# Graph network on one core: GpSimd's gathers wait for VectorE's additions and are spaced by progress

## What is computed

```python
q = (h @ Wq.T + bq)[dst]; k = (h @ Wk.T + bk)[src]; v = (h @ Wv.T + bv)[src]      # by head
alpha = jnp.sum(q * k, axis=-1) / sqrt(D_HEAD)
ex = jnp.exp(alpha - segment_max(alpha, dst)[dst])
a = ex / (segment_sum(ex, dst)[dst] + 1e-16)
out = segment_sum((a[:, :, None] * v).reshape(-1, f), dst)
# then a gate with x_r = h @ Ws.T + bs, a layer norm, and a feed-forward of 512 with gelu
...
msg = silu(concat([x[src], x[dst], rbf]) @ mw1 + mb1) @ mw2 + mb2                  # last pass
agg = segment_sum(msg, dst) / max(cnt, 1)
out = silu(concat([x, agg]) @ uw1 + ub1) @ uw2 + ub2                              # and layer norms
```

## Time and profile before

| | |
|---|---|
| median of 3 runs | 5662.24 us (5661.85 to 5665.38) |
| profiled execution: its span | 7864.5 us |
| its time beside the span | not shown; the page gives the span alone |
| busy share of the span | PE 58%, VectorE 52%, GpSimd 49%, ScalarE 35% |
| DMA | 536.12 MB, of it 490.24 MB by GpSimd's queue |
| chain that ended last | PE 27%, unknown 25%, issue 20%, VectorE 17% |

### The profile page before, as it was taken

One profiled execution on the slowest core, in us unless ns is written; L12 is line 12 of the kernel. 1 busy time (PEld: TensorE's weight loads), 2 busy tenths in 40 slices (PEclk: granted clock), 3 DMA queues, 4 the chain that ended last, 5 costly groups with the idle time before them and its releaser, 6 DMA issues.

```text
span 7864.5 us, 105863 instructions
## 1 busy us (share of the span) xinstructions
PE 4591.8 (58%) x22799; PEld 3687.8 (47%) x22800; DVE 4054.1 (52%) x11127; ACT 2762.9 (35%) x6393; POOL 3848.5 (49%) x4061
## 2 busy tenths in 40 slices
PE   4555555655555556555555565555555655666666
PEld 2444444534444445344444453444444544555555
DVE  4555555645555556455555564555555653333334
ACT  1333333423333334233333342333333432333333
POOL 3555555335555553345555543455555425555553
PEclk6666666676666666766666667666666677878788
DMA  4222222122222222222222222222222211111111
GB/s 127 78 78 74 78 78 77 52 66 76 78 77 79 76 79 57 65 69 77 77 79 77 79 61 68 68 78 78 78 76 80 60 31 44 44 45 45 45 44 27
DMA packets 267185, 536.12 MB, mean 68 GB/s; under 512 B 116251, under 2 KB 148687, under 8 KB 266507
## 3 DMA queue, kind: packets, MB, share of 16 engines
q0 software_dynamic: 180992, 490.24, 23.2%
q1 hardware_dynamic: 78899, 35.89, 1.8%
q10 hardware_dynamic: 6936, 6.69, 0.3%
HBM read 512.41 MB, written 18.03 MB: 67 GB/s over the span
## 4 chain that ended last, share of the span: by engine, by line
PE 27%; another core or an unknown queue 25%; issue 20%; DVE 17%; ACT 5%; DVEq 4%; ACTq 1%; DMA 0%; SPq 0%; POOL 0%; POOLq 0%
PE bank L765 9%; PE bank L784 8%; DVE acc L1191 6%; PE bank L769 2%; PE bank L756 2%; ACT oh L549 2%; DVEq L330 2%; PE bank L805 2%; PE bank L833 1%; DVE alpha L1214 1%; DVEq L1191 1%; DVE slots L1283 1%; DVE oh L1175 1%; PE bank L937 1%
## 5 line engine op out<-in xcount | busy, mean ns | idle before, releaser
L504 POOL DMA_INDIRECT slots<-kv_table,idx x3224 | 3065.0, 951 | 3149.1 <-PE bank L784 1272.7
L784 PE MATMUL bank<-slots,oh 128*128 128x136 f32 (+1 forms) x8060 | 1598.6, 352 | 584.7 <-DVE acc L1191 502.7
L765 PE MATMUL bank<-qs,ohT 128*128 x8080 | 1676.3, 354 | 230.3 <-ACT ohT L540 132.0
L784 PEld LDWEIGHTS bank<-slots,oh 128*128 128x128 f32 x8060 | 1415.4, 253 | 716.9 <-DVE acc L1191 614.8
L765 PEld LDWEIGHTS bank<-qs,ohT 128*128 128x128 f32 x8080 | 1428.7, 256 | 450.4 <-issue 428.3
L1191 DVE TENSOR_TENSOR acc<-acc,bank 128x136 f32 (+1 forms) x4030 | 1173.6, 291 | 603.7 <-PE bank L784 166.4
L1208 DVE TENSOR_TENSOR slots<-slots,bank 128x512 f32<-128x512 f32 x808 | 552.3, 684 | 1312.1 <-remote 1294.4
L540 ACT ACTIVATE ohT<-bank,miss 128x512 f32<-128x512 f32 x1010 | 676.5, 683 | 1360.0 <-PE bank L756 1226.6
L504 POOL DMA_INDIRECT slots<-src_table,idx x806 | 760.8, 944 | 750.5 <-DMA idx<-src_e 233.6
L549 ACT ACTIVATE oh<-iota,rel_e 128x128 f32<-128x128 f32 x3168 | 962.9, 387 | 0.0
L797 PE MATMUL bank<-ident,alpha 128*128 128x128 f32 x204 | 93.7, 459 | 1459.5 <-DVE alpha L1214 1423.0
(11 more groups left out here) (255 smaller groups left out, 4032.7 us busy)
## 6 DMA issues: line engine op xcount, KB each, us to landing
slots<-kv_table,idx POOLq DMA_INDIRECT x3224
kv_table<-slots SPq DMA_DIRECT2D x20, 660.0 KB, 3.4
slots<-src_table,idx POOLq DMA_INDIRECT x806
resets<-flat_len ACTq DMA_DIRECT2D x51, 128.0 KB
idx<-src_e SPq DMA_DIRECT2D x255, 8.0 KB
terms<-flat_rel SPq DMA_DIRECT2D x255, 12.0 KB
resets<-flat_rst SPq DMA_DIRECT2D x2, 1551.0 KB
w<-in_w SPq DMA_DIRECT2D x8, 256.0 KB
```

Of the source, the lines that this page charges most:

```text
L504: pool.indirect_dma_start(slots[:, k, t, 0:width], None, table, bass.IndirectOffsetOnAxis(ap=idx[:, k, t:t + 1], axis=0))\
L765: mm = pe.matmul(o, ohT[:, j % 2, t, :], qs[:, blocks[j * G + t], 0:HID], start=True, stop=basis is None)
L784: mm = pe.matmul(bank[6 + part % 2][:, o:o + width], oh[:, k % 2, t, :], slots[:, k, t, HID:HID + width], start=True, stop=True)
```

## The change

GpSimd no longer waits for `slot_free`, which is gone; TensorE announces all six parts by `part_ps` and VectorE waits for that. GpSimd counts `acc_done` instead: group 0 of chunk c waits for 4 additions of chunk c-4, group 1 for 12, groups 2 and 3 for 16, and group 3 also for `spread_used` 10 products past the start of chunk c-4, which is the second product of chunk c-2. In layers 1 to 3 (`headed`) the first four chunks are paced too: chunk 0's groups 1 to 3 wait for 7, 14 and 21 query additions, chunk 1's group 0 for all 25 and group 1 for the cleared accumulator, chunk 2's groups 0 and 2 for the layer's first product and first carries, chunk 3's groups 0 and 2 for 4 and 12 additions of chunk 0. The waits for the table stay with the first four chunks.

```diff
-            def gather_chunk(k, turn, l, table, width, places=CH):
...
-                        pool.wait_ge(slot_free[k][j], START + used[j])
-                        pool.reg_add(uses[k][j], uses[k][j], 1)
+            def paced(s, value, done, step):
+                pool.wait_ge(s, START + value + pool.snap(done))
+                pool.reg_add(done, done, step)
+            def paced_head(k, j):
+                if k == 0 and j > 0:
+                    paced(q_ev, 7, asked, 7)
+                elif k == 1 and j == 0:
+                    paced(q_ev, NB - 21, asked, NB - 21)
+                elif k == 1 and j == 1:
+                    paced(acc_zero, 1, zeroed, 1)
+                elif k == 2 and j == 0:
+                    paced(spread_used, 1, first_used, NG * CHUNKS)
+                elif k == 2 and j == 2:
+                    paced(carries_packed, 1, packed, CHUNKS)
+                elif k == 3 and j == 0:
+                    paced(acc_done, G, begun, 2 * G)
+                elif k == 3 and j == 2:
+                    paced(acc_done, G, begun, CH * CHUNKS - 2 * G)
+            def await_added(before, j, chunks):
+                pool.wait_ge(acc_done, START + (G, CH - G, CH, CH)[j] + before[j])
+                pool.reg_add(past[j], past[j], CH * chunks)
+                if j == NG - 1:
+                    paced(spread_used, 2 * NG + 2, ahead, NG * chunks)
+            def gather_chunk(k, l, first, headed, table, width, places=CH, to_next=(1,) * NG):
...
                 for j in range(groups):
+                    if headed:
+                        paced_head(k, j)
+                    if not first:
+                        await_added(before, j, to_next[j])
...
-                    if t % G == G - 1 or (last and t == LAST_PLACES - 1):
-                        mm.then_inc(slot_free[k][j], 1)
-                    elif t == end - 1:
-                        mm.then_inc(part_ps, len(WITHIN) if last else 1)
+                    if t == end - 1:
+                        mm.then_inc(part_ps, len(PARTS) - part if last and part == parts[-1] else 1)
...
-                if t == first and (end % G == 0 or (last and end == LAST_PLACES)):
-                    j = (end - 1) // G
-                    dve.wait_ge(slot_free[k][j], START + turn_of(l, i, k, j) + 1)
-                elif t == first:
-                    dve.wait_ge(part_ps, START + len(WITHIN) * g + WITHIN.index(part) + 1)
+                if t == first:
+                    dve.wait_ge(part_ps, START + len(PARTS) * g + (len(PARTS) if last and part == LAST_PARTS[-1] else part + 1))
```

More of the change, by code:

```diff
@@ L71 @@
 assert PARTS[LAST_PARTS[-1]][1] == LAST_PLACES and len(LAST_PARTS) > 1
-assert LAST_HALVES == 1 and LAST_PARTS[0] in WITHIN and LAST_NG > 1
+assert LAST_HALVES == 1 and LAST_NG > 1
 assert NB % BW == 0 and REM > 1 and FULL % ROUNDS == 0
@@ L265, in build_program @@
         kv_in = [sems(f"kv_in{k}_", NG) for k in range(RING)]
-        slot_free = [sems(f"slot_free{k}_", NG) for k in range(RING)]
         oh_far = sem("oh_far")
@@ L289, in build_program @@
                    scale_done, shift_done, shift_spread, silu_done, spread_used, sq_done, t_in,
-                   t_out, t_ps, w_done,
-                   *[s for ring in slot_free for s in ring]]
+                   t_out, t_ps, w_done]
         def is_last(i, k):
@@ L482, in _ @@
                                         bass.IndirectOffsetOnAxis(ap=vti[:, c:c + 1], axis=0)).then_inc(su_rows, 16)
[L483 to L486, removed]
-            def gather_chunk(k, turn, l, table, width, places=CH):
-                groups = -(-places // G)
[L490 to L496, removed]
-                for j in range(groups):
-                    if isinstance(turn, int):
-                        pool.wait_ge(slot_free[k][j], START + turn)
-                    else:
-                        pool.wait_ge(slot_free[k][j], START + used[j])
-                        pool.reg_add(uses[k][j], uses[k][j], 1)
+            past = [pool.alloc_register(f"past{j}") for j in range(NG)]
@@ new lines, in _ @@
+            staged = [pool.alloc_register(f"staged{k}") for k in range(RING)]
+            ahead, asked, zeroed, first_used, packed, begun = [
+                pool.alloc_register(name) for name in ("ahead", "asked", "zeroed", "first_used", "packed", "begun")]
+            for r in (*past, *staged, ahead):
+                pool.reg_mov(r, 0)
+            for r, of_layer in ((asked, NB), (zeroed, 1), (first_used, NG * CHUNKS), (packed, CHUNKS), (begun, CH * CHUNKS)):
+                pool.reg_mov(r, of_layer)
@@ new lines, in await_added @@
+            def await_added(before, j, chunks):
[4 more added lines that the diff above has]
+            def gather_chunk(k, l, first, headed, table, width, places=CH, to_next=(1,) * NG):
+                groups = -(-places // G)
+                before = [pool.snap(past[j]) for j in range(groups)]
+                if first:
+                    if k == 2:
+                        pool.wait_ge(su_termsd, 48)
+                    if k == 3:
+                        pool.wait_ge(su_rstd, 16 * 2 * HEADS)
+                    pool.wait_ge(tab_out, 16 * NI * (l + 1))
+                pool.wait_ge(idx_in[k], 16 + pool.snap(staged[k]))
+                pool.reg_add(staged[k], staged[k], 16)
+                for j in range(groups):
+                    if headed:
+                        paced_head(k, j)
+                    if not first:
+                        await_added(before, j, to_next[j])
@@ L506, in gather_chunk, with gather_pass @@
                             .then_inc(kv_in[k][j], 16)
-            def gather_rest(l, table, width):
-                for k in range(REM):
[L510 to L520, removed]
+            def gather_pass(l, table, width, headed):
+                for k in range(RING):
+                    gather_chunk(k, l, True, headed, table, width)
+                with pool.Fori(1, FULL):
+                    for k in range(RING):
+                        gather_chunk(k, l, False, False, table, width)
+                for k in range(REM):
+                    places = min(CH, PLACES - (RING * FULL + k) * CH)
+                    ends = [k == (REM - 1 if j < LAST_NG else REM - 2) for j in range(NG)]
+                    gather_chunk(k, l, False, False, table, width, places,
+                                 [CHUNKS - (RING * FULL + k - RING) if end else 1 for end in ends])
+            gather_pass(0, kv_table, KVW, False)
+            with pool.Fori(1, L) as l:
+                gather_pass(l, kv_table, KVW, True)
+            gather_pass(L, src_table, HID, False)
+            for passed in past:
+                pool.wait_ge(acc_done, START + pool.snap(passed))
+            pool.wait_ge(spread_used, START + pool.snap(ahead))
             def root(sums, out, nth):
@@ L1350, in message_step @@
                 if ahead > 1:
-                    dve.wait_ge(slot_free[k][1], START + turn_of(L, i, k, 1) + 1)
+                    dve.wait_ge(part_ps, START + len(PARTS) * g + 3)
                     onehots(n + 1, k, c + 2, 0, LAST_HALVES if is_last(i, k + 2) else 2)
```

1 line of the change is left out of this document (removed).

## The result

| | before | after |
|---|---|---|
| median | 5662.49 us (4 runs, 5661.85 to 5665.38) | 5688.29 us (4 runs, 5683.88 to 5688.95) |
| ratio | | 1.0045, 95% interval 1.0032 to 1.0057 |
| profiled execution | span 7864.5 us | span 5682.1 us, time 5683.88 us |

The change costs 26 us, 0.45%. The forecast was no change.

The account below looks back on a forecast made before the run. The prediction took GpSimd's gathers, 1.25 us apart, as the bound (sum 5622 us). Every part of the change was priced at 0, so the forecast stayed at the runs' median, 5662 us, range 5550 to 5720.

Parts of the forecast that it names:

- TensorE and VectorE: Announcing all six product parts by part_ps leaves matmuls, additions and VectorE's waits in number and order: 0 us.
- GpSimd as the bound: Untraced, gathers 1.25 us apart set the time: 5 x 806 gathers plus the stretches around them sum to 5622 us.
- Compute alone: Time without waiting on GpSimd: 18.9 us a chunk in layers, 17.0 in the last pass, about 5345 us in sum.
- The new waits of GpSimd: Waits for VectorE's additions and second product are met when reached: 0 us; 306 us if no register steps were covered.
- clearing the accumulator: Estimated 4 us in the heads of layers 1 to 3, after the query additions.
- landing: Estimated 3 us for the last gather's data to arrive, used for the stretches between gather stages.
- The stand: VectorE's product on line 1208 waits 6.75 us at a time, 1294.4 us in the first trace; removal worth 0 untraced.
- groups of four with gaps: Expected sign in the changed kernel's trace: a gap behind every four gathers, line 1208's wait more than halved.
- what comes late is TensorE's signal: VectorE's product on line 1208 waits for its fetch and TensorE's queries alone; the data is not late.
- The stand is partly real: Faster rival: untraced gathers take well under 1.25 us; spacing gives 5345 to 5504, weak form 5622 to 5650; chance 27%.
- The paced head idles GpSimd: Slower rival: chunks 2 and 3 of layers 1 to 3 wait, costing 25 us up to 189; chance 20%.
- slow query additions: In the heads, additions 1.22 us apart would delay gathers 8 us a layer, 25 in all, giving 5687.

Follow-up runs that it names:

- the run with 12 gathers: Kernel before with every group's fourth gather left out, 12 a chunk instead of 16, slots filled once ahead of layer 0: 5417.78 us, ratio 0.9561.

## Why the prediction was wrong

**The step that failed** is this one: "*TensorE and VectorE.* Before, two of the six parts of the products are announced by slot_free and four by part_ps; after, all by part_ps. Matmuls, additions and VectorE's waits keep their number and order: 0." Number and order do stay. But one wait changed the event it waits for, from place 7 to place 8, and TensorE does 6.6 us of other work between these. That costs 26 us (5685.58 against 5659.61 with this edit alone in the kernel before; 5660.52 for the changed kernel without it). I had priced `slot_free` as GpSimd's semaphore and the parts' announcement, and missed its third reader, VectorE's one-hots (line 1351 of the kernel before), which the description of that kernel leaves out too.

**GpSimd as the bound held.** The sum of 5622 fell short of the unstalled span of 5658.7 by 37 us: gathers 5051 (1012.7, 1010.7, 1009.7, 1010.6, 1007.2) for 5037, the stretches between 491 (120.0, 119.9, 119.3, 131.9) for 471, the end 63.6 for 61. Compute alone was put at 5345 us; the run with 12 gathers, less the 18 us of filling, spans 5397, its 19.2 us a chunk being 0.3 above the 18.9 that I had read from the end of a layer.

**The new waits of GpSimd** cost 0 as said, 4025 gaps of 0.30 us, and so do the paced heads (5687.01 without them). Two estimates of the prediction had no row: clearing the accumulator, 4 us, takes 2.9 (the row at 1199.35), and landing, 3 us, takes 2.8 from the issue (the changed kernel's page).

**The stand** was rightly taken out of the timed runs. The first reason given, that GpSimd's own sum explains the time, held. The second is not shown: it put the stand down to tracing, by the Trainium skill (NOTIFIC — the notification-queue block, "Overflow: three behaviours, one of which stalls the engine"), for a trace path that holds its producer back. The page states that of the block's internal pipeline; of a full ring it states, under "The overflow → `NRT_EXEC_SW_NQ_OVERFLOW` path", that the runtime lets the record be discarded. Ten of the eleven traces here have spans within 2 us of their times, so tracing as such does not bring the stand, and no run shows whether that path held an engine in the eleventh. The forecast that the changed kernel's profile would show groups of four with gaps and a span of 6600 to 7500 us fell with it: 5682.1, no gaps.

To the prediction's "what comes late is TensorE's signal" belongs a row of the same trace, the query matmuls for the product of the earlier trace rows:

```profile
327.24 1.05 PE L765 MATMUL bank<-qs,ohT 128*128 x8
```

They end at 328.3, and the product starts at 335.83. So the rows show no late work on TensorE. As the ends of matmuls are modelled, they do not tell whether the end or only the signal came late, and what held it stays open.

**The rivals.** "The stand is partly real" is refuted by the kernel before, traced again: 1.25 us a gather, no stand, and 5660.48 us. "The paced head idles GpSimd" named the right side with the wrong place; that its 25 us for slow query additions (5687) come within 2 us of the measured time is luck, for the heads cost nothing. The time lies within the range, 5550 to 5720, and belongs to none of the cases that made it: that, too, is luck.

## What to carry to other kernels

When a semaphore is replaced, list every wait that reads it, and for each ask which instruction raises the new one and what its engine does between the old event and the new; a signal one matmul later can be a whole group of work later. A bound engine hides such a slip only up to its own period, so price the chain alone and subtract the cover. If a profile's span is far from the timed runs, trace once more before reading stages from it.

## What was not expected of the hardware

One of two executions of the kernel before that were traced had a stand of some 7 us at a time and took 1.39 times its usual length, with the same program and data; nothing that was varied here (lead, gathers in a row, spacing, pacing) brought it back, in one trace each.
